# Branch sum to third norm by halves of the tokens in a fused FFN, attention and FFN kernel on one Trainium2 core

## The reference

```python
# four branches of each token and head, weighted by a softmax gate w, summed
# o  = w0*f_short + w1*f_long + w2*delta + w3*v        (64 numbers for each of 4 heads)
# o  = o / sqrt(mean(o*o) + 1e-5) * onorm_w
# x2 = x1 + o @ Wo
# y  = x2 + 0.5 * (gelu(layernorm(x2) @ w1 + b1) @ w2 + b2)
def _layernorm(x, axis=-1, eps=1e-05):
    m = jnp.mean(x, axis=axis, keepdims=True)
    v = jnp.var(x, axis=axis, keepdims=True)
    return (x - m) / jnp.sqrt(v + eps)
```

## Time and profile before

| | |
|---|---|
| time, median of 3 runs | 1204.77 us |
| the profiled execution's own time | 1207.12 us |
| its span | 1205.4 us |
| PE busy | 1053.0 us (87%) |
| DVE busy | 821.7 us (68%) |
| ACT busy | 548.9 us (46%) |
| POOL busy | 414.4 us (34%) |
| mean granted TensorE clock | 0.936 of full |

### The profile page before, as it was taken

One profiled execution on the slowest core, in us unless ns is written; L12 is line 12 of the kernel. 1 busy time (PEld: TensorE's weight loads), 2 busy tenths in 40 slices (PEclk: granted clock), 3 DMA queues, 4 the chain that ended last, 5 costly groups with the idle time before them and its releaser, 6 DMA issues.

```text
span 1205.4 us, 25681 instructions
## 1 busy us (share of the span) xinstructions
PE 1053.0 (87%) x10348; PEld 779.9 (65%) x10348; DVE 821.7 (68%) x1556; ACT 548.9 (46%) x965; POOL 414.4 (34%) x648
## 2 busy tenths in 40 slices
PE   3938898899989998899988998899988998897738
PEld 2823784488637884488637885488637885487427
DVE  6584477875787577875787667865787567863363
ACT  2244338443655337443564337443564337532322
POOL 8118200950058200951048300861048300860000
PEclk9968899999999999999999999999999999995758
DMA  5140104020220103020230203110130202120000
GB/s 156 19 105 2 35 18 96 11 52 2 69 55 11 43 19 89 18 48 6 51 74 3 51 19 73 33 35 20 44 80 1 53 1 68 39 51 3 1 0 18
DMA packets 82933, 47.45 MB, mean 39 GB/s; under 512 B 58496, under 2 KB 76416, under 8 KB 82816
## 3 DMA queue, kind: packets, MB, share of 16 engines
q1 hardware_dynamic: 82816, 45.82, 16.4%
HBM read 31.12 MB, written 14.68 MB: 38 GB/s over the span
## 4 chain that ended last, share of the span: by engine, by line
PE 59%; DVE 25%; ACT 7%; issue 4%; POOL 3%; DMA 1%; SPq 0%; DVEq 0%; ACTq 0%; POOLq 0%
PE psum L789 12%; PE psum L791 11%; PE psum L790 11%; DVE conv_acc L1374 6%; PE psum L820 4%; DVE arena L1607 3%; PE psum L982 3%; PE psum L967 3%; PE psum L1001 2%; PE psum L1006 2%; PE psum L1161 2%; ACT arena L587 2%; DVE arena L1609 2%; DVE f_fm L1504 1%; POOL l_prod L525 1%
## 5 line engine op out<-in xcount | busy, mean ns | idle before, releaser
L525 POOL TENSOR_TENSOR l_prod<-arena 64x30 f32<-64x30 f32 (+14 forms) x240 | 150.3, 626 | 568.5 <-DMA arena<-l_dram 550.3
L583 ACT ACTIVATE h_f<-psum,b_col 128x512 f32<-128x512 f32 x128 | 87.9, 688 | 209.4 <-PE psum L791 209.2
L529 POOL TENSOR_TENSOR arena<-arena,l_prod 64x30 f32<-64x30 f32 (+14 forms) x240 | 157.0, 654 | 18.8
L1088 PE MATMUL psum<-v_shift,fir_w 128*32 128x512 f32 x1152 | 143.9, 622 | 13.5 <-DVE wo_lo L1250 13.5
L789 PE MATMUL psum<-w_hi,h_hi 128*128 128x256 f32 x512 | 149.7, 292 | 0.0
L791 PE MATMUL psum<-w_hi,h_lo 128*128 128x256 f32 x512 | 143.6, 280 | 0.0
L790 PE MATMUL psum<-w_lo,h_hi 128*128 128x256 f32 x512 | 143.5, 280 | 0.0
L1374 DVE SCALAR_TENSOR_TENSOR conv_acc<-psum,conv_col,conv_acc 128x511 f32<-128x511 f32 x144 | 107.7, 748 | 32.0 <-ACT conv_acc L608 20.8
L789 PE MATMUL psum<-xt_hi,w_hi 128*128 128x512 f32 x256 | 109.6, 428 | 14.5 <-DVE b_half L1467 7.1
L1353 DVE CAST h_hi<-h_f 128x512 fp32r<-128x512 f32 x128 | 62.1, 485 | 88.1 <-PE psum L791 40.8
L820 PE MATMUL psum<-ident,arena 128*128 128x128 f32 x384 | 57.4, 298 | 54.7 <-DVE arena L1621 35.1
(11 more groups left out here) (232 smaller groups left out, 2198.3 us busy)
## 6 DMA issues: line engine op xcount, KB each, us to landing
x_in<-in_L_attn_x SPq DMA_DIRECT2D x8, 512.0 KB, 3.8
v_dram<-v_fm SPq DMA_DIRECT2D x16, 256.0 KB, 2.8
v_shift<-v_dram SPq DMA_DIRECT2D x16, 256.0 KB, 3.6
out<-x_tok SPq DMA_DIRECT2D x8, 512.0 KB, 2.9
v_shift<-v_dram SPq DMA_DIRECT2D x16, 255.5 KB, 4.4
v_shift<-v_dram SPq DMA_DIRECT2D x16, 255.0 KB, 5.2
v_shift<-v_dram SPq DMA_DIRECT2D x16, 254.5 KB, 5.8
arena<-in_L_ffn_w SPq DMA_DIRECT2D x2, 1024.0 KB, 7.2
```

The source lines that it names most:

```text
L525: pool.tensor_tensor(prod, l_inv[:, k + 1:, k:k + 1].broadcast_to(shape), l_inv[:, k:k + 1, 0:k].broadcast_to(shape), ALU.mult).then_inc(i ...
L529: pool.tensor_tensor(l_inv[:, k + 1:, 0:k], l_inv[:, k + 1:, 0:k], prod, ALU.add).then_inc(inverted, 1)
L583: act.activation(h_f[:, m % 2, :], bank, ACT.Gelu, bias=b1_col[:, m:m + 1]).then_inc(read, 1)
L1088: last = pe.matmul(fir[p][0][col:col + 32, :], fir_w[:, group, n - 1 if n else TAPG, :], v_shift[:, group, at_t:at_t + T], start=(n < 2), ...
```

## The change

The whole stretch from the branch sum to the third norm is done by halves of the tokens (two tiles, eight units), and the first half goes ahead of the second half's sum. On DVE the three 2048-element steps become six of 1024, the 1024-element sum becomes two of 512, and the reduction, root, reciprocal, variance and normalisation are done twice over half the columns. The order of the queues changes too: DVE takes the input statistics (`row_stats(x_in)`) into the place where it waited for Exp, their aggregation (`variances(0, ...)`) between the halves, and `q_rows` and `q_inverse` later; ACT takes the roots by halves, with `root(0)` ahead of the FIR copies and the `v_t` and `f_t` copies ahead of the third norm's roots; PE puts `v_t` between the two halves of `mix_t`, and three of the four `f_t` between the two halves of `wo`.

```diff
-        DVE_STEPS = {"head": 49, "body": 82, "last": 77, "tail": 38}
+        DVE_STEPS = {"head": 49, "body": 90, "last": 85, "tail": 46}
...
+                    mix_square(at, 0)
+                    mix_root(at, 0)
+                    mix_square(at, 1)
+                    mix_root(at, 1)
+                    high_rows(at, 3, "mix_t", 0)
+                if at.next:
+                    root(0, j + 1)
                 if at.front:
                     for h in range(2, HEADS):
                         out_of(at, "fir", h, f_fm[:, h, :])
                     act.sem_inc(fir_done, 1)
...
                 if at.back:
-                    for b in range(2):
-                        pe.wait_ge(norm_made, 2 * i + b + 1)
-                        turn_tiles(at, "mix_t", b)
...
+                if at.back:
+                    mixed_rows(0)
                 if at.front:
                     firs(at, 1, range(8, 9))
...
+                    weighted(f_tok, 0, 0)
+                    summed = branch_sum(0, weighted(dv_tok, 2, 0))
+                    weighted(f_tok, 0, 1)
+                    mixed(0, summed)
+                    weighted_d = weighted(dv_tok, 2, 1)
+                    mean_square(0)
+                    summed = branch_sum(1, weighted_d)
+                    mix_normalise(0)
+                    mixed(1, summed)
+                    mean_square(1)
+                if at.next:
+                    variances(0, range(TILES), x_rows)
+                if at.back:
+                    mix_normalise(1)
+                    low_rows(3, "mix_t", 0)
+                if at.front:
+                    q_rows()
+                if at.back:
+                    low_rows(3, "mix_t", 1)
+                if at.back:
+                    dve.wait_ge(x2_begun, i + 1)
+                    residual_rows(0)
+                    residual_rows(1)
+                if at.front:
+                    q_inverse()
+                if at.back:
+                    ln3_normalise(0)
+                    ln3_normalise(1)
+                    low_rows(2, "ln3", 0)
+                    low_rows(2, "ln3", 1)
```

More of the change, by code:

```diff
@@ L757, in one_pass @@
                     act.sem_inc(fir_done, 1)
-                if at.next:
-                    root(0, j + 1)
                 if at.back:
-                    root(2, i)
+                    high_rows(at, 3, "mix_t", 1)
                 if at.front:
@@ L1177, in one_pass, with mixed_rows, output @@
                     firs(at, 1, range(0, 8))
+                def mixed_rows(b):
+                    pe.wait_ge(norm_made, 2 * i + b + 1)
+                    turn_tiles(at, "mix_t", b)
+                def output(b):
+                    copied(pe, at, "mix_t", b)
+                    bank, full = claim(pe, at, "wo", b)
+                    for t in (2 * b, 2 * b + 1):
+                        for k in range(HALVES):
+                            rows = slice(P * t, P * t + P)
+                            last = product3(pe, bank[:, C * (t % 2):C * (t % 2) + C], xt_hi[:, k, rows], xt_lo[:, k, rows],
+                                            wo_hi[:, k, :], wo_lo[:, k, :], k == 0, k == HALVES - 1)
+                    last.then_inc(full, 1)
@@ L1178, in one_pass, with fir_rows @@
+                def fir_rows(t):
+                    turn(at, "f_t", t, lambda h: f_fm[:, h, P * t:P * t + P])
                 if at.back:
-                    for b in range(2):
-                        pe.wait_ge(norm_made, 2 * i + b + 1)
-                        turn_tiles(at, "mix_t", b)
+                    mixed_rows(0)
                 if at.front:
                     firs(at, 1, range(8, 9))
+                    to_tok(at, "v_t", lambda h: v_fm[:, h, :])
                 if at.back:
[L1185 to L1193, removed]
+                    mixed_rows(1)
+                    output(0)
@@ L1194, in one_pass @@
                 if at.front:
-                    to_tok(at, "v_t", lambda h: v_fm[:, h, :])
                     copied(pe, at, "fir", HEADS - 1)
-                    for t in range(TILES):
-                        turn(at, "f_t", t, lambda h: f_fm[:, h, P * t:P * t + P])
+                    for t in range(TILES - 1):
+                        fir_rows(t)
+                if at.back:
+                    output(1)
+                if at.front:
+                    fir_rows(TILES - 1)
                     off_diagonal(at, "lhalf")
@@ L1339, in low, with low_rows @@
                         dve.sem_inc(next_ready, 1)
[L1341 to L1347, removed]
+                def low_rows(k, what, b):
+                    bank, read = arrive(dve, at, what, b)
+                    dve.wait_ge(xhi_made[k], 2 * i + b + 1)
+                    cols = slice(2 * P * b, 2 * P * b + 2 * P)
+                    dve.tensor_tensor(xt_lo[:, :, cols], bank.rearrange("p (h t) -> p h t", h=HALVES),
+                                      xt_hi[:, :, cols].bitcast(F32), ALU.subtract).then_inc(read, 1)
                 def split(f, seq, m):
@@ L1611, in one_pass @@
[L1611 to L1620, removed]
+                    units = [slice(2 * HEADS * b, 2 * HEADS * b + 2 * HEADS) for b in range(2)]
@@ L1621, in one_pass, with mix_normalise @@
+                    def mix_normalise(b):
+                        us = units[b]
+                        dve.wait_ge(oroot_made, 2 * i + b + 1)
+                        link(dve.reciprocal(oinv[:, us], onrm[:, us]))
                         dve.tensor_tensor(xn_u[:, us, :], f_tok[:, us, 0, :],
                                           oinv[:, us].unsqueeze(2).broadcast_to([P, 2 * HEADS, D]), ALU.mult).then_inc(norm_made, 1)
[L1623 to L1632, removed]
+                    def residual_rows(b):
                         bank, read = arrive(dve, at, "wo", b)
@@ L1646, in one_pass @@
[L1646 to L1653, removed]
+                        tiles = range(2 * b, 2 * b + 2)
```

109 lines of the change are left out of this document (75 added, 34 removed).

## The result

| | before | changed |
|---|---|---|
| time, median | 1204.8 us (4 runs, 1200.77 to 1205.9) | 1223.24 us (4 runs, 1222.44 to 1227.96) |
| ratio | | 1.0161, 95% interval 1.0138 to 1.0183 |
| span of the profiled execution | 1205.4 us | 1226.2 us |
| mean granted TensorE clock in it | 0.936 | 0.926 |

I had forecast 1203.5 with a range of 1194 to 1211. What came is beyond the range, in the direction of rival C and 9 us past its price. The profiled execution of the changed kernel, 1227.96 us, is its slowest of four.

A forecast was written before the change was run, and what follows sets the result against it. DVE's queue, with short handoffs to ACT and PE, was taken to bound the stretch. Bodies -1.0, last pass +0.3 and tail -0.6 gave -1.3 us on the 1204.77 median: 1203.5, range 1194 to 1211.

The forecast's parts named there:

- rival C: Slower: clock falls around v_t and again at ln3, second half of wo late, 1.4 us more a body, 1214; chance 0.13.
- PE's 2.67 us: PE's wait ahead of the first mix_t; 0.1 to 0.4 would be left, with 1.8 us moved behind v_t.
- rival B: PE's idle time is simply gone, 2.3 us kept at each mix_t: 18 us less, 1186; chance 0.08.
- A body pays for one clock drop: Each body has one fall of PE's clock to 1.2 GHz, early (behind the mix_t wait) or late (on ln3 and attend).
- the change saves that much only if it has none: An early clock drop, behind the wait at mix_t, is worth 0.94 us a body, saved only without one.
- the early fall: Clock drop behind PE's 2.67 us wait ahead of mix_t, from 498.3 to about 501.6; worth 0.94 us a body.
- 0.4 + 1.8 us of idle time: PE's forecast waits around v_t: up to 0.4 ahead of the first mix_t, 1.8 ahead of the second.
- The late fall: Clock drop on ln3 and attend, expected in four of six bodies, 1.1 us each.
- The halves' own cost: Splitting DVE's big steps: 0.15 us a split, nine added instructions, about 1.35 us more DVE work.
- F - W: Time from first weighted multiply (W) to second FFN's first matmul (F): 28.81 us before, 27.9 forecast without clock drop.
- The input statistics: 1.39 us of DVE work moved into its wait for Exp: gain 1.3 us, 0.8 in the first and sixth bodies.
- The tail: Second FFN's first matmul at 1174.8 to 1175.3 instead of 1175.59; taken as 0.6 us less.

The follow-up runs named there:

- b9: Kernel before plus unread idle transposes on PE ahead of logits, first mix_t, key products, and in the tail ahead of mix_t and ln3: 1197.05 us, ratio 0.9928.
- e6: Changed kernel plus unread idle transposes on PE ahead of ln3 alone (18 and 5): 1209.44 us, ratio 1.0034 to the kernel before.
- e5: Changed kernel plus 14 unread idle transposes on PE ahead of the second mix_t alone: 1214.49 us, ratio 1.0071 to the kernel before.
- e1: Changed kernel plus unread idle transposes on PE ahead of the second mix_t (14) and ln3 (18 and 5): 1203.01 us, ratio 0.9971 to the kernel before.
- e7: Kernel before with only the next sequence's input statistics moved into DVE's wait for Exp: 1207.82 us, ratio 1.0014.

## Why the prediction was wrong

- **What bounds the stretch** was read rightly: DVE's queue with PE's clock falls on top. That PE's 2.67 us could not simply be won was right too, rival B was far off. "A body pays for one clock drop" overlooks another one in each body of the kernel before, 10 to 16 us ahead of W, in the middle one at 474.4; b9 takes it away with the rest, and what it costs by itself no run shows.

```profile
475.00:476.00 1.00, 1.00 (x4) 0.50 0.61 242
```

- **The step that failed** is "the change saves that much only if it has none": I let the early fall go in the likeliest case and gave it 13 in 100 as rival C, because 0.4 + 1.8 us of idle time is less than 2.67 + 0.33. The waits were 0.84 and 1.94 (here even the places were right), and five of the six bodies had the fall. The sum holds nothing for it, where alone it costs 1.3 us (e6). I priced a wait by its length when the rows of before already showed that length alone doesn't decide: 2.29 us led to a fall and 2.48 did not.
- **The late fall** was expected in four of six bodies; it came in all six and in the last pass. I priced it at 1.1 us, with a length of 3.3 us taken from the early fall. For a fall of 3.4 us that was right (0.7 to 1.1 in e5). But in four bodies and the last pass it lasted 6.8 us and cost 2.3, half of that or more behind F, where I had put nothing.
- **The sum.** I had 5.1 us for falls (four late ones at 1.1 and 0.7 in the last pass). Against e1 they cost 18.6. That is some 14 of the 22 us between the forecast (1.3 less) and the two spans (20.8 more). Some 5 of the rest are the order itself, which follows, and 3 are the last row of the table of stretches.
- **The halves' own cost** was mis-sized. In the third body the six half-size steps come to 8.5 us where I had 7.8, and the two 512-element sums to 2.0 where I had 1.5. I took a split at 0.15 us from the tail, where POOL is idle; beside POOL the two big multiplies took 5.0 us whole and four half-size ones 6.0. The first `mix_t` came 11.2 behind W against my 10.7, the second 15.8 against 14.9, and F - W without any fall 28.6 and not 27.9. In the last pass it is 28.2 in e1 where I had 26.9.
- **Rival C** named the mechanism: both falls, `wo` late, DVE waiting for it ahead of a residual. It gave 1214 for 1.4 us a pass; measured from W to the next merge it is 1.7 to 3.5. Its price lacked the 6.8 us falls and the slower steps.
- **The input statistics** cost or gave nothing by themselves (e7).
- **The tail** gained 1.36 us from W to F; I had 0.6.
- The Trainium skill's rule of the oscillating clock ("TensorE: Matmul & The Clock Gate", HAM oscillation), half of the time spent cold, gives 1.7 us for a fall of 3.4 and 3.4 for one of 6.8 (estimates by that page). Measured are 0.7 to 1.3 and 2.3, so for one fall it is too high here, probably because a part of the slow work hides behind DVE's queue. That its 19 us for the 37.5 us more at the lower level come near the 20.8 between the spans is in part luck, since the slower DVE steps and the 3 us outside the stretch are in the 20.8 as well.

## What to carry to other kernels

Where an engine other than PE sets the pace of a stretch, moving PE's idle time around changes what the clock does, and that can cost more than the order gains: count the falls of the granted clock and what stands under each, before and after. A few transposes that nobody reads, placed in the known waits, tell how much of a loss is the clock, if the kernel before gets them too (here it gained 5 us as well), and here they also made the fastest kernel. A fall is cheapest on work that hides behind another engine: the early one cost 0.6 us with both halves of `wo` together and 1.3 with three `f_t` between them, and a late one costs most where it reaches into the FFN.

## What the runs showed of the hardware that was not expected

In the changed stretch falls of the granted clock came in two lengths, 3.4 and 6.8 us, the longer ones also while PE was busy throughout (241 to 246 us of the changed kernel's trace). Nearly the same wait led to a fall in one body and to none in the next: 1.91 to 1.98 us in five bodies of the changed kernel did, 2.08 in its fourth did not, and in e6 1.99 did once and 1.99 to 2.05 in four bodies did not.

In the bodies, with POOL busy beside them, DVE's multiplies of 1024 elements took 1.40 to 1.55 us and the sums 1.21 to 1.39; in the tail, where POOL is idle, both took 1.22 to 1.23. POOL's small products took as long as the DVE step beside them (spans on POOL are rough): the same 64x150 product 2.42 us beside steps of 2048 elements in the kernel before, and 1.35 beside steps of 1024 in the changed kernel.

```profile
487.20 2.42 POOL L525 TENSOR_TENSOR l_prod<-arena 64x150 f32<-64x150 f32 x1
```

```profile
494.87 1.35 POOL L525 TENSOR_TENSOR l_prod<-arena 64x150 f32<-64x150 f32 x1
```
